# Summing two accumulators at the end of an attention and mixture-of-experts kernel: by POOL's adder, or by accumulating DMAs

## The reference

```
x = x + cross_attention(layernorm(x), ctx)      # 16 heads of 64, 64 keys
xf = layernorm(x)                               # 4096 rows
idx = top_2(softmax(xf @ gate_w.T) + gate_b)    # of 8 experts
y  = sum over the two experts e of  score_e * expert_e(xf)
z  = shared_expert(xf)
out = x + y + z                 # expert: silu((x@w1+b1) * (x@w3+b3)) @ w2 + b2, hidden 352
```

## Time and profile before

| | us |
|---|---|
| median of 3 runs | 730.51 |
| the runs | 729.13, 730.51, 735.97 |
| the profiled execution | 740.14 |
| its span, first to last instruction | 738.4 |
| mean granted TensorE clock, share of full speed | 0.968 |

### The profile page before, as it was taken

One profiled execution on the slowest core, in us unless ns is written; L12 is line 12 of the kernel. 1 busy time (PEld: TensorE's weight loads), 2 busy tenths in 40 slices (PEclk: granted clock), 3 DMA queues, 4 the chain that ended last, 5 costly groups with the idle time before them and its releaser, 6 DMA issues.

```text
span 738.4 us, 16760 instructions
## 1 busy us (share of the span) xinstructions
PE 676.5 (92%) x4582; PEld 629.8 (85%) x4583; DVE 535.3 (72%) x1106; ACT 402.5 (55%) x1308; POOL 431.3 (58%) x514
## 2 busy tenths in 40 slices
PE   4997699999999989975698899999999999999986
PEld 3786499998888879875698899999999999999985
DVE  3855688888977878766988766666666666666796
ACT  3965777777766766764563434444444444444432
POOL 5344474545458777665346327667776777776281
PEclk9978899999999999996999999999999999999999
DMA  8201223336525776543641325554444444455694
GB/s 242 84 1 43 87 62 96 101 94 185 184 73 126 169 156 127 119 119 88 152 81 41 75 43 74 75 73 71 71 74 71 75 74 74 73 93 101 146 408 182
DMA packets 76549, 79.03 MB, mean 107 GB/s; under 512 B 21690, under 2 KB 70180, under 8 KB 76484
## 3 DMA queue, kind: packets, MB, share of 16 engines
q1 hardware_dynamic: 56980, 54.71, 27.4%
q0 software_dynamic: 15760, 18.96, 15.7%
q10 hardware_dynamic: 3744, 4.59, 1.8%
HBM read 47.22 MB, written 31.01 MB: 106 GB/s over the span
## 4 chain that ended last, share of the span: by engine, by line
PE 70%; DMA 7%; issue 7%; SPq 6%; DVE 5%; POOL 4%; ACT 1%; ACTq 0%; DVEq 0%; POOLq 0%
PE ps L1249 58%; DMA slots_scratch<-record,slot 5%; PE ps L1346 3%; PE ps L1426 3%; SPq L539 3%; SPq L540 3%; POOL slots_scratch L664 2%; PE ps L1418 2%; PE ps L1323 1%; DMA wq_sb<-in_L_xattn_Wq 1%; PE ps L1336 1%; DMA xrow<-xn_scratch,slots 1%; DVE st L1069 1%; PE ps L1374 1%; DVE x L1067 1%
## 5 line engine op out<-in xcount | busy, mean ns | idle before, releaser
L721 POOL DMA_INDIRECT acc_scratch<-yrow,slots x71 | 112.7, 1588 | 77.0 <-ACT yrow L910 56.5
L910 ACT ACTIVATE yrow<-ps,slots 128x256 f32<-128x256 f32 x71 | 33.7, 474 | 147.8 <-PE ps L1249 133.2
L1249 PE MATMUL ps<-AU,xTh 128*128 128x512 f32 x256 | 98.6, 430 | 8.6 <-DVE xTl L1047 8.6
L1249 PE MATMUL ps<-AU,pTh 128*128 128x256 f32 x512 | 101.3, 290 | 0.0
L1175 DVE TENSOR_TENSOR uv<-ps,b 128x704 f32<-128x704 f32 x71 | 63.3, 892 | 48.1 <-PE ps L1249 44.7
L1249 PE MATMUL ps<-w13h,uxTh 128*128 x284 | 97.7, 344 | 0.0
L1249 PE MATMUL ps<-w13h,uxTl 128*128 x284 | 91.6, 322 | 0.0
L1249 PE MATMUL ps<-w13l,uxTh 128*128 x284 | 91.3, 322 | 0.0
L664 POOL DMA_INDIRECT slots_scratch<-record,slot x64 | 67.5, 1054 | 40.6 <-DMA slots_scratch<-record,slot 26.5
L714 POOL DMA_INDIRECT xrow<-xn_scratch,slots x71 | 69.7, 982 | 26.8 <-issue 21.7
L1249 PEld LDWEIGHTS ps<-AU,pTh 128*128 128x128 f32 x512 | 82.3, 191 | 0.0
(11 more groups left out here) (239 smaller groups left out, 2002.5 us busy)
## 6 DMA issues: line engine op xcount, KB each, us to landing
sums<-acc_scratch SPq DMA_DIRECT2D x16, 512.0 KB, 11.4
w_raw<-in_L_ffn_w SPq DMA_DIRECT2D x16, 352.0 KB, 4.0
xin<-in_x SPq DMA_DIRECT2D x32, 128.0 KB
xres<-in_x SPq DMA_DIRECT2D x32, 128.0 KB
acc_scratch<-x SPq DMA_DIRECT2D x32, 128.0 KB
xn_scratch<-xn SPq DMA_DIRECT2D x32, 128.0 KB
xn2T_scratch<-xn2T SPq DMA_DIRECT2D x32, 128.0 KB
xrow<-xn2T_scratch SPq DMA_DIRECT2D x32, 128.0 KB
```

The costliest lines, as they stand in the source:

```text
L721: pool.indirect_dma_start(acc_dram[u % 2], bass.IndirectOffsetOnAxis(ap=slots[:, u, 0:1], axis=0), yrow[:, m % YRING, :], None, compute_op ...
L910: act.activation(yrow[:, y, :], ps[:, 6 + m % 2, 0:D], ACT.Copy, scale=slots[:, bass.ds(u, 1), 1].bitcast(F32)).then_inc(y_ok, 1)
L1249: last = pe.matmul(out, stationary(k, a), moving(k, b), start=(k == 0 and i == 0), stop=(k == n - 1 and i == len(PARTS) - 1 and not more))
```

## The change

SP loads only acc0's rows, 8 DMAs in place of 16, and `sums` is half as large. POOL waits for y_out as SP does, then for each quad waits for SP's load and issues one DMA on its own queue that reads acc1's rows from DRAM and adds them to `sums` in SBUF (512 KB each, 4 KB a row). The adder is no longer used. Its semaphore is gone too: the accumulation of quad q signals the ring semaphore q of the gathers, renamed `pool_in`, whose value after the last gather is known (`both_in`). SP's outputs and DVE's additions wait for that.

```diff
         tail = ExitStack()
-        sums = sb("sums", [P, 2, NT // QUAD, QUAD, D], F32, tail)
+        sums = sb("sums", [P, NT // QUAD, QUAD, D], F32, tail)
...
-        gather_in = [sem(f"gather_in{i}") for i in range(RING)]
+        pool_in = [sem(f"pool_in{i}") for i in range(RING)]
...
+        def both_in(q):
+
+            return 16 * len([u for u in range(NU) if (R0 + u) % RING == q]) + 16
...
             for q in range(NT // QUAD):
                 b, j = divmod(q * QUAD, TPB)
-                for i in range(2):
-                    sp.dma_start(sums[:, i, q, :, :], acc_tiles[i][:, b, j:j + QUAD, :]).then_inc(sums_in[q], 16)
+                sp.dma_start(sums[:, q, :, :], acc_tiles[0][:, b, j:j + QUAD, :]).then_inc(sums_in[q], 16)
             for q in range(NT // QUAD - 1):
                 b, j = divmod(q * QUAD, TPB)
                 if q < NA // QUAD:
-                    sp.wait_ge(both_ok, q + 1)
+                    sp.wait_ge(pool_in[q], both_in(q))
...
+            pool.wait_ge(y_out[0], 16 * len(range(0, NU, 2)))
+            pool.wait_ge(y_out[1], 16 * len(range(1, NU, 2)))
             for q in range(NT // QUAD):
-                both = [sums[:, i, q, :, :].rearrange("p a d -> p (a d)") for i in range(2)]
-                pool.wait_ge(sums_in[q], 32)
-                pool.tensor_tensor(both[0], both[0], both[1], ALU.add).then_inc(both_ok, 1)
+                b, j = divmod(q * QUAD, TPB)
+                pool.wait_ge(sums_in[q], 16)
+                pool.dma_start(sums[:, q, :, :], acc_tiles[1][:, b, j:j + QUAD, :], accum_op=ALU.add).then_inc(pool_in[q], 16)
...
-                    dve.wait_ge(both_ok, NT // QUAD)
+                    dve.wait_ge(pool_in[NT // QUAD - 1], both_in(NT // QUAD - 1))
...
-                    dve.wait_ge(both_ok, q + 1)
+                    dve.wait_ge(pool_in[q], both_in(q))
```

More of the change, by code:

```diff
@@ L364, in xattn_moe @@
         sums_in = [sem(f"sums_in{q}") for q in range(NT // QUAD)]
-        both_ok = sem("both_ok")
         out_ok = sem("out_ok")
@@ L562, in _ @@
                 if q < NA // QUAD:
-                    sp.wait_ge(both_ok, q + 1)
+                    sp.wait_ge(pool_in[q], both_in(q))
                 else:
                     sp.wait_ge(out_ok, q - NA // QUAD + 1)
-                sp.dma_start(out_tiles[:, b, j:j + QUAD, :], sums[:, 0, q, :, :]).then_inc(all_out, 16)
+                sp.dma_start(out_tiles[:, b, j:j + QUAD, :], sums[:, q, :, :]).then_inc(all_out, 16)
             for i in range(QUAD):
                 sp.wait_ge(last_ok, i + 1)
-                sp.dma_start(out_tiles[:, B - 1, TPB - QUAD + i, :], sums[:, 0, NT // QUAD - 1, i, :]).then_inc(all_out, 16)
+                sp.dma_start(out_tiles[:, B - 1, TPB - QUAD + i, :], sums[:, NT // QUAD - 1, i, :]).then_inc(all_out, 16)
             sp.wait_ge(all_out, 16 * (NT // QUAD - 1 + QUAD))
@@ L714, in gather @@
                 pool.indirect_dma_start(xrow[:, m, :], None, xn2_dram,
-                                        bass.IndirectOffsetOnAxis(ap=slots[:, u, 0:1], axis=0)).then_inc(gather_in[m], 16)
+                                        bass.IndirectOffsetOnAxis(ap=slots[:, u, 0:1], axis=0)).then_inc(pool_in[m], 16)
             def scatter_add(u):
@@ L1146, in unit_step @@
                 if isinstance(t, int) and t >= RD:
-                    row = sums[:, 0, NT // QUAD - 1, t - RD, :]
-                    dve.wait_ge(both_ok, NT // QUAD)
+                    row = sums[:, NT // QUAD - 1, t - RD, :]
+                    dve.wait_ge(pool_in[NT // QUAD - 1], both_in(NT // QUAD - 1))
                     dve.wait_ge(Y_ok, t + 1)
@@ L1185, in unit_step @@
                     z0 = (q - NA // QUAD) * QUAD
-                    row = sums[:, 0, q, :, :].rearrange("p a d -> p (a d)")
-                    dve.wait_ge(both_ok, q + 1)
+                    row = sums[:, q, :, :].rearrange("p a d -> p (a d)")
+                    dve.wait_ge(pool_in[q], both_in(q))
                     dve.wait_ge(z_row_ok, z0 + QUAD)
@@ L1414, in unit_step @@
                 if is_routed(t, routed):
-                    wait(pe, gather_in[m], 16 * ((t - R0) // RING) + 16)
+                    wait(pe, pool_in[m], 16 * ((t - R0) // RING) + 16)
                     wait(pe, uxTl_ok, t)
```

## The result

The changed kernel took 748.1 us (median of 4 runs, 745.7 to 749.9), the kernel before 731.8 beside it; the ratio is **1.018**, with a 95% interval of 1.014 to 1.022. The two medians alone lie 16.3 us (2.2%) apart. The ratios in this document leave out a kernel's executions of a second, slower kind, over 1.5% above its fastest. The profiled execution took 749.9 us, with a span of 748.1; it was the longest of the four.

The account below looks back on a forecast made before the run. PE was taken to bound the whole, with 5.7 us lost at the end to POOL's additions. Accumulations landing at 734.2, plus 11.3 and 1.5, gave 747.0, +8.6 us on the 730.5 median: 739.1 us, range 726 to 751.

Parts of the forecast that it names:

- What bound the end before: In the last 45 us, POOL's additions hold DVE's instructions with two SBUF operands and PE waits: 5.7 us lost.
- POOL's DMA issues don't hold DVE: POOL's eight DMA issues, 0.8 us each, were priced at 0 for DVE; 0 to 3 us if they held it.
- The price of an accumulating 4 KB packet: Each 4 KB row added into sums was taken at 330 ns, twice a plain one, between ends of 164 and 528.
- the scatter's excess: The 1 KB scatter-adds cost 88 ns over plain rows: 44 taken to grow with size, 44 as a delay others fill.
- The start of the accumulations: Accumulation 0 was to enter the DMA engines at about 700.3, after load 0 landed and POOL's 0.8 us issue.
- The pairing: Two queues alternate packet by packet on each DMA engine: 64 pairs of 330 + 165 ns, 31.7 us.
- The landing of accumulation 7: The last accumulation lands at 734.2, where DVE waits for it at the first addition of the last four tiles.
- The tail: From the first addition of the last four tiles to the end: 11.3 us, plus 1.5 for slow clock (0 to 2.7).
- The sum: End of the kernel at 747.0 against 738.4, +8.6 us, carried over to a median of 739.1 us.
- my likeliest part: An accumulating packet of 265 to 430 ns, giving 734.9 to 745.6 us for the kernel; chance 0.45.
- rival 2: The whole accumulation excess grows with size, 430 to 528 ns a packet: 745.6 to 751.8 us; chance 0.20.
- nearly the plain price: Rival in which an accumulating packet costs 165 to 265 ns; at 165 the kernel takes 727.0 us; chance 0.27.

Follow-up runs that it names:

- no_second: Changed kernel without POOL's eight accumulating DMAs and its two waits, so acc1's rows are never added: ratio 0.986 to the kernel before.
- outs_last: Changed kernel with SP's outputs of quads 0 to 4 held until the last accumulation has landed: ratio 1.006 to the kernel before.
- acc_rows_1k: Changed kernel with each accumulating DMA cut into four with 1 KB rows: 50.6 us from anchor to end against 48.2 in the changed kernel, one run.
- acc_ordered: Changed kernel with loads, accumulations and outputs in the order of quads 5, 6, 7, then 0 to 4: ratio 0.999 to the kernel before.
- plain_copy: Changed kernel with POOL's eight DMAs copying acc1's rows over sums instead of adding them: ratio 0.999 to the kernel before.

## Why the prediction was right, and where it was off

- **What bound the end before**: right. no_second gives the 5.7 us back, and with POOL's additions in quarters the steps are 3.3 to 3.4 us long again. In a second profile of the same kernel the loss is 8.5.
- **POOL's DMA issues don't hold DVE**: right, L1161 stays at 0.42 to 0.43 us beside 0.87 us issues.
- **The price of an accumulating 4 KB packet**: right, 328 to 331 ns against 330 taken, but not for all the reasons given. I took half of the scatter's excess for a delay that other packets fill. At 4 KB there is no such filling (a plain row beside the accumulations costs its full 164 ns, see outs_last), and acc_rows_1k has an excess of 16 ns, not 44. The Trainium skill gives the halving for the adding step of a ring collective, ReduceScatter (Collectives: The Full Stack, "The bandwidth ceiling: the fold count and why AG ≠ RS ≠ AR"). The rates here, DRAM to SBUF at 4 KB, agree with it: 211 GB/s against 410. That the two source reads are the reason no run here shows.
- **The start of the accumulations**: a term that I put at nothing. I let accumulation 0 enter the engines as soon as POOL had issued it, 5.8 us after SP's first load (700.3 - 694.46). Its first packet came 10.8 us after it (702.2 - 691.45): POOL began to issue at 5.3, the first issue took 0.96 us, and then q0 stayed empty for 4.5 us. Other first issues beside full DMA engines show the same lag: 3.4 us in acc_ordered, 3.7 in plain_copy, 4.5 in outs_last, and in the kernel before 4.0 us for L624, whose issue ended at 9.7 while q0 had its first packet at 13.7. So it could have been read beforehand. The last scatter-add of the kernel before, issued from 690.73 to 692.28 with the engines nearly empty, had rows moving before 693. What makes the lag is open.
- **The pairing**: about right. From its first packet to its last, at about 732, the queue took 29.8 us for its 64 rows an engine, 0.47 each instead of 0.495. During the lag the loads ran alone, so they were through by about 712, not 722, and fewer plain rows were left to take turns (0.87 for each accumulating row from 718 to 731.5); and an accumulating row took 312 ns of an engine, not 330.
- **The landing of accumulation 7**: mis-sized by the sum of these, 42.4 us from SP's first load (691.45 to 733.85) instead of 39.7 (694.46 to 734.2). That the times 726.3 and 734.2 nearly stand in the profile (726.38 and 733.85) is luck: this execution reached its first load 3.0 us earlier than the one before.
- **The tail**: mis-sized. 14.3 us instead of 11.3 + 1.5, since the clock stayed at the lower level for all of it; the upper end that I gave (+ 2.7) was close.
- **The sum**: 2.7 + 1.5 us on top of the 8.6 make 12.8, and the first two profiles differ by 12.9 from the anchor; the ratio of 1.018 is 13.2 us of 731.8. By the profiled spans it would have been 9.7 us.
- **Where 748.1 lies**: inside the range of 726 to 751, but beyond my likeliest part (734.9 to 745.6) and in the numbers of rival 2, whose mechanism did not happen: it needed 430 ns or more, and 328 were measured. Of the 9.0 us above my 739.1, 4.3 are the two mis-sized terms and 1.3 the median of the kernel before (731.8 for 730.5). The remaining 3.4 are the difference between medians and profiles, and no term of mine explains them.
- **The rivals**: "nearly the plain price" would have needed what plain_copy shows, a landing 11.4 us earlier; the rest fell with the price.

## What to carry to other kernels

An accumulating DMA pays for its addition with DMA time: here twice the time of a plain transfer of the same rows, taken from every other transfer on the engines. It also starts late beside full engines, here 3.4 to 4.5 us after its issue. It is worth it where the DMA engines have slack and nobody waits for the result; where they are full, first order the transfers by who waits (acc_ordered took back all of the 1.8%). And POOL's additions stretched DVE instructions with both operands in SBUF from 0.43 to 2.5 us, though the two worked on different tensors, so price an off-loaded addition by the instructions that meet it, too.

## What I had not expected

- A two-operand instruction of DVE held through eight POOL additions in a row (5.52 us, 0.53 alone), once, where in the other profiles it got in after one.
- A DMA of POOL that had been issued for some 4 us before its first packet moved, with the DMA engines full.
- The clock after an idle stretch: in the changed kernel and in plain_copy it stayed at 0.50 for the whole tail of some 14 us, with PE busy for about 70% of it in short pieces (2.93 of 4 us), while in outs_last it was back at 1.00 from 730 on:

```profile
726.00:730.00 4.00, 2.93 (x12) 2.53 (x12) 3.30 (x6) 0.65 (x2) 0.00 (x0) 0.58 0.96 380
730.00:734.00 4.00, 2.34 (x17) 2.11 (x18) 1.41 (x3) 0.71 (x2) 0.00 (x0) 1.00 1.02 401
```

  The length of PE's idle time ahead of the tail does not order them: 15.9 us in the changed kernel and 4.4 in plain_copy, where the clock stayed down, and 8.5 in outs_last, where it came back:

```profile
721.79 0.58 PE L1253 MATMUL ps<-ws2h,hTh 128*128 128x256 f32 x1 [4.38 <-DVE hTl L1166]
...
726.38 0.58 PE L1255 MATMUL ps<-ws2h,hTh 128*128 128x256 f32 x1 [8.46 <-DVE hTl L1168]
```

  What decides between them is open; no run was made for it.
- A change of 0.5% needed 12 runs in this kernel, since the first 440 us alone move the anchor by 12 us between executions. The distance from an anchor in the profile needs fewer, but one is not enough for less than some 3 us: it was 35.3 and 38.0 in two profiles of the same kernel.
